# Two dense feed-forward stages as eight fixed slots on four banks, started inside the Fourier attention

## The chip, the cores and the metric

The kernel runs on one core of a Trainium2 chip. The metric is the device time of one execution in microseconds (us); the median of three runs of the kernel before is 939.75 us (938.83 to 942.45).

## The reference, cut to what matters

Four layers, each an attention part and a feed-forward part, act on a sequence of 2048 tokens of 128 features, in fp32. The change touches the end of the last layer: its attention uses Fourier features, and two dense feed-forward networks of 512 hidden units follow, each behind a layer norm.

```python
# layer 3, attention part (x is layer-normed before it, and normed again inside)
p = einsum('blhd,dm->blhm', q_or_k, proj_mat) / sqrt(D_HEAD)
features = concatenate([cos(p), sin(p)]) / sqrt(D_KMAP)       # for keys and for queries
attended = linear_attention(features_q, features_k, v) @ wo + bo
z = z + attended                                              # z: the inner residual
# dense network 1: ln2 with its gain and bias, w1 128x512, w2 512x128
z = z + relu(ln(z) @ w1 + b1) @ w2 + b2
x = x + z
# layer 3, feed-forward part: dense network 2
x = x + relu(layernorm(x) @ W1 + b1) @ W2 + b2                # W1 128x512, W2 512x128
```

## The kernel before, in words

**Tiling.** The 2048 tokens are four chunks of 512 (`NC = 4`, `CH = 512`). All activations stay in SBUF: `X` and `Z` hold the residuals with tokens on partitions, `XH` and `XL` the normed input turned (features on partitions). Every matmul operand is split into a rounded high part (fp32r) and a low remainder, and a product is three matmuls of 128x128 by 128x512 (`mm3`, L695 to L697): high by high, high by low, low by high.

**Stages.** The order of work is written out by hand. `STAGES_` names ten stages, `slots()` runs each over the four chunks, and each engine walks the same list (`walk` for TensorE, ScalarE and VectorE, a loop of its own for GpSimd). A stage's body has named points at which the norm steps of a chunk that is needed two chunks later and the tail of the chunk before are put in; for four-block stages `STEPS_AT[4]` says where. Each engine runs its list strictly in order and waits on semaphores.

**The last Fourier products.** `lin_pe`, `lin_act` and `lin_dve` work through 64 pairs of feature blocks (`PALL = 64`): phases into `gate_banks` or `up_banks`, rounding and subtracting on VectorE (L1606), two Sin activations (L1616, L1617), and products into `route_bank` or `spread_bank` (L1557). After the last pair ScalarE copies the bank out (`output_act`, L1747), VectorE splits it (`project_dve`), TensorE multiplies by `wo3` into `y_bank` (`project_pe`), and ScalarE writes `YT` (`project_act`, L1757). At the end of `lin_pe` and `lin_act` this is done for the last chunk before the next stage begins.

**The dense stages before (FFN3, FFN4).** Each has four hidden blocks of 128 for each chunk (`ffn_pe`, `ffn_act`, `ffn_dve`, `ffn_pool`). A block is: up product into `G[n % 2]` (the two halves of `gate_banks`); ScalarE Relu with bias into `AO[n % 2]` (L864); VectorE CAST to the high part in `rbuf` (L924); GpSimd, and VectorE for the last two blocks of a stage, subtract to get the low part (`low`, L949); down product into `y_bank`, two blocks behind the up product (`lag = 2`). After four blocks ScalarE writes `YT` (`result`, L878), TensorE turns it in four 128x128 transposes into `norm_bank` (`TN`; `tail_pe`, L709), and VectorE adds it to `Z` and `X` (`tail_dve`, L717 to L722). The two sets of everything (two banks, two `AO`, two high and two low buffers) bind a block to the block two before it.

**The norm of a chunk.** Statistics of `Z` or `X` on VectorE (L375, L378), the reciprocal root on GpSimd (L477, L478), normalising into `XN` on VectorE (L395, step 1), four transposes into `norm_bank` (`front_pe`, L662, step 2), a copy to `X32` on ScalarE (L499 with scale and bias, L502 without), then the split into `XH` and `XL` on VectorE (L410, L412, step 3). Norms and tails share `norm_bank`, so the transposes of a norm wait until VectorE has added the tail before (`res_done`), and those of a tail wait for the `X32` copy of the norm before.

## Time and profile before

| | us |
|---|---|
| median of three runs | 939.75 |
| lowest, highest | 938.83, 942.45 |
| the profiled execution's own time | 939.33 |
| its span (first to last instruction) | 937.5 |
| TensorE busy | 749.5 (80%) |
| VectorE busy | 694.7 (74%) |
| ScalarE busy | 553.9 (59%) |
| GpSimd busy | 429.6 (46%) |

The profile shows one execution. A busy share is an average over ten stages with different limits. The granted TensorE clock is given as a share of full speed, and it has two levels, 1.2 and 2.4 GHz; its mean over the span is 0.891. The last Fourier products end shortly before 848.5 us, and the dense stages take the rest of the span.

### The profile page before, as it was taken

What the parts mean: (1) busy time and instruction counts of PE and PEld (TensorE: products, weight loads), DVE (VectorE), ACT (ScalarE), POOL (GpSimd) and SP (SyncE); (2) the same over time, 40 slices, a digit from 0 to 9 for tenths busy, and PEclk for the clock granted to TensorE, in tenths of its full rate; (3) what the DMA queues carried; (4) which work ended last, traced back from release to release, by engine and by line L of the source; (5) the groups of instructions that cost most, each with busy time, mean ns of one, the idle gap of its engine ahead of it and who ended that gap; (6) DMA issues with size and microseconds to landing.
All of it is one profiled execution on the core that took longest, in us unless ns stands there. A gap on an engine that the chain in (4) does not pass through costs nothing. (4 is left out here: it accounts for less than half of the span.)

```text
span 937.5 us, 10990 instructions
## 1 busy us (share of the span) xinstructions
PE 749.5 (80%) x3306; PEld 474.2 (51%) x3306; DVE 694.7 (74%) x1644; ACT 553.9 (59%) x877; POOL 429.6 (46%) x463
## 2 busy tenths in 40 slices
PE   4788996898988799886579888868677867767776
PEld 3566763454655577764456665633232222224554
DVE  6686875989896377776766667778888778784675
ACT  5254664746745356543136666768799887784333
POOL 6547655454442045556426766624433123303554
PEclk9998999979877689999769999978899888898799
DMA  4100000001000000001000000000000000000001
GB/s 137 58 12 15 23 15 25 23 16 31 23 8 11 1 1 1 0 1 34 1 0 1 1 1 0 1 0 1 1 1 0 1 1 0 1 1 0 1 0 46
DMA packets 9610, 11.59 MB, mean 12 GB/s; under 512 B 720, under 2 KB 5712, under 8 KB 9552
## 3 DMA queue, kind: packets, MB, share of 16 engines
q1 hardware_dynamic: 9552, 10.89, 4.0%
q8 instruction: 27, 0.44, 0.2%
q14 instruction: 31, 0.25, 0.1%
HBM read 9.84 MB, written 1.05 MB: 12 GB/s over the span
## 5 line engine op out<-in xcount | busy, mean ns | idle before, releaser
L949 POOL TENSOR_TENSOR rbuf<-B,rbuf 128x512 fp32r<-128x512 f32 x154 | 200.6, 1305 | 175.6 <-ACT rbuf L872 111.2
L917 DVE TENSOR_TENSOR B<-B,spread_bank 128x512 f32<-128x512 f32 x128 | 87.1, 682 | 45.2 <-ACT B L864 35.2
L872 ACT ACTIVATE rbuf<-B 128x512 fp32r<-128x512 f32 x132 | 82.9, 628 | 41.5 <-PE y_bank L697 32.4
L695 PE MATMUL y_bank<-rbuf,WH 128*128 128x512 f32 x174 | 75.5, 434 | 29.8 <-POOL rbuf L949 18.8
L864 ACT ACTIVATE B<-gate_banks,WR 128x512 f32<-128x512 f32 x96 | 66.0, 688 | 39.1 <-PE gate_banks L697 29.0
L904 DVE TENSOR_TENSOR B<-B,up_banks 128x512 f32<-128x512 f32 x68 | 46.5, 684 | 49.0 <-PE up_banks L697 30.1
L861 ACT ACTIVATE B<-gate_banks 128x512 f32<-128x512 f32 x68 | 40.8, 599 | 64.6 <-PE gate_banks L697 63.5
L695 PE MATMUL gate_banks<-XH,WH 128*128 128x512 f32 x168 | 75.5, 450 | 2.5 <-ACT YT L1273 0.8
L477 POOL TENSOR_SCALAR small<-small 128x4 f32<-128x4 f32 x36 | 7.5, 209 | 141.0 <-DVE small L378 140.4
L697 PE MATMUL y_bank<-rbuf,WL 128*128 128x512 f32 x174 | 70.2, 404 | 0.0
L696 PE MATMUL y_bank<-rbuf,WH 128*128 128x512 f32 x174 | 70.2, 404 | 0.0
L697 PE MATMUL gate_banks<-XH,WL 128*128 128x512 f32 x168 | 70.0, 417 | 0.0
L696 PE MATMUL gate_banks<-XL,WH 128*128 128x512 f32 x168 | 70.0, 416 | 0.0
L1616 ACT ACTIVATE B<-B,VEC 128x1024 f32<-128x1024 f32 x48 | 55.3, 1151 | 22.4 <-DVE B L1611 22.3
L1163 POOL TENSOR_SCALAR B<-S,WR 128x128 f32<-128x128 f32 x64 | 39.1, 627 | 50.2 <-DVE S L1145 38.0
L1518 POOL TENSOR_SCALAR WH<-WK 128x512 fp32r<-128x512 f32 x22 | 13.8, 628 | 105.3 <-issue 57.9
L695 PEld LDWEIGHTS y_bank<-rbuf,WH 128*128 128x128 f32 x174 | 33.9, 195 | 55.7 <-POOL rbuf L949 28.7
L1204 PEld LDWEIGHTS spread_bank<-VB,B 128*128 128x128 f32 x256 | 38.2, 229 | 35.7 <-issue 26.5
L823 PE MATMUL spread_bank<-SCT,WE 128*128 128x512 f32 x96 | 42.5, 443 | 11.1 <-DVE B L917 9.2
L1617 ACT ACTIVATE B<-B 128x1024 f32<-128x1024 f32 x48 | 50.5, 1053 | 0.0
L1181 PE MATMUL gate_banks<-B,S 128*64 128x512 f32 x128 | 44.7, 788 | 6.8 <-issue 3.8
L662 PE MATMUL norm_bank<-WR,XN 128*128 128x128 f32 x128 | 22.5, 304 | 32.4 <-DVE XN L395 24.0
(290 smaller groups left out, 2060.3 us busy)
## 6 DMA issues: line engine op xcount, KB each, us to landing
STG<-in_w_split SPq DMA_DIRECT2D x27, 256.0 KB, 2.7
X<-in_x SPq DMA_DIRECT2D x4, 256.0 KB, 6.0
out<-X SPq DMA_DIRECT2D x4, 256.0 KB, 2.3
WR<-in_w_raw SPq DMA_DIRECT2D x1, 524.5 KB, 5.5
STG<-in_w_exact SPq DMA_DIRECT2D x2, 256.0 KB, 2.7
STG<-in_w_split SPq DMA_DIRECT2D x5, 64.0 KB, 1.9
STG<-in_w_split SPq DMA_DIRECT2D x1, 192.0 KB, 2.3
STG<-in_w_split SPq DMA_DIRECT2D x1, 128.0 KB, 2.1
```

Source lines behind the costliest of these rows:

```text
L695: nc.tensor.matmul(dst, w[0], x[0], start=start, stop=False)
L696: nc.tensor.matmul(dst, w[0], x[1], start=False, stop=False)
L697: return nc.tensor.matmul(dst, w[1], x[0], start=False, stop=stop)
L823: nc.tensor.matmul(SP[:, :], WE[:, o:o + P], SCT[:, bass.ds(c % 2 * CH, CH)], start=True, stop=True).then_inc(spread_full, 1)
L864: nc.scalar.activation(AO[n % 2], G[n % 2][:, :], ACT.Relu, bias=raw(bias, b, 1))\
L872: nc.scalar.activation(rbuf[n % 2][:, :], HO[n % 3], ACT.Copy).then_inc(hh_ready, 1)
L904: nc.vector.tensor_tensor(MO[n % 2], AO[n % 2], U[n % 2][:, :], ALU.mult).then_inc(mul_done, 1)
L917: nc.vector.tensor_tensor(HO[n % 3], src, SP[:, :], ALU.mult).then_inc(h_ready, 1)
L949: e_.tensor_tensor(rbuf[2 + n % 2][:, :], AO[n % 2] if f.dense else HO[n % 3], rbuf[n % 2][:, :].bitcast(F32), ALU.subtract).then_inc(hl_r ...
L1181: i = nc.tensor.matmul(G[u][w * WIN:(w + 1) * WIN, :], QN[c_ % 2][:, tok], KM[tile % 2][:, HU * u:HU * u + HU, w * WIN:(w + 1) * WIN], sta ...
L1616: nc.scalar.activation(CS[p % 4], AB[p % 4], ACT.Sin, scale=-TURN, bias=half_pi).then_inc(cos_ready, 1)
L1617: nc.scalar.activation(SN[p % 4], RB[p % 4], ACT.Sin, scale=-TURN).then_inc(sin_ready, 1)
```

## The change

FFN3 and FFN4 leave the general `ffn_` functions. Eight slots of their own (`ring3`, `ring4`; j = 0 to 7) take their place, one for each chunk of each stage, with blocks numbered k = 0 to 31 throughout.

- Up products go round four banks (`UPD`: both halves of `gate_banks` and `up_banks`), and high parts, plain activations and low parts have four buffers each (`HID`, `AOD`, `LOD`); the down product runs three blocks behind, and the output alternates between `spread_bank` and `y_bank` (`YD`).
- ScalarE reads the up bank twice: Relu straight to the rounded high part (`HID`), then Relu in fp32 (`AOD`). The CAST on VectorE is gone. VectorE subtracts for three blocks of a slot and GpSimd for the fourth (VectorE for all four in the last two slots).
- Each slot has one fixed order for norm and tail: on TensorE four blocks, then the norm's transposes, then the tail's; on VectorE low 0, statistics, low 1, the split of the norm before, normalising, low 2, low 3 where it has it, tail.
- The first two up products are issued ahead of the last Fourier products, the next two behind them, and the attention's last projection and its copy move into slot 0.
- Norms from (7, 2) on are turned in `route_bank` (`R`) instead of `norm_bank`; the wait on `res_done` goes, and the tails no longer wait for these norms' `X32` copies.

```diff
-    _f.lag = 2 if _f.dense else 3
+    _f.lag = 3
+        def norm_bank(n, c):
+            return R if count(n, c) >= count(7, 2) else TN
...
-                if turned["tails"]:
+                if norm_bank(n, c) is R:
+                    pe.wait_ge(oq_read, NC)
+                elif turned["tails"]:
                     pe.wait_ge(res_done, turned["tails"])
...
-                pe.wait_ge(x32_ready, turned["norms"])
+                pe.wait_ge(x32_ready, min(turned["norms"], count(7, 2)))
...
+                if p == PALL - 1:
+                    for k in range(2):
+                        ring_up(pe, k)
                 lin_use(pe, p)
...
-            if cp == 2 * NC - 1:
-                project_pe(pe, NC - 1)
...
                 output_act(a, NC - 1)
-                project_act(a, NC - 1)
...
+        DEEP, RB4 = 4, 4
+        UPD = [G[0], G[1], U[0], U[1]]
+        AOD = [buf[0], buf[1], buf[2], buf[3]]
+        HID = [SCT[:, 0:CH], SCT[:, CH:2 * CH], rbuf[2][:, :], rbuf[3][:, :]]
+        LOD = [WE[:, 0:CH], WE[:, CH:2 * CH], rbuf[0][:, :], rbuf[1][:, :]]
+        YD = [SP, Y]
+        SLOTS = 2 * NC
...
+        def ring_front(j):
+            return divmod(count(7, 2) + j, NC) if count(7, 2) + j < count(9, 0) else None
+        def ring_tail(j):
+            return divmod(count(6, NC - 1) + j, NC)
+        def ring_low_on_pool(k):
+            return k % RB4 == 3 and k // RB4 < SLOTS - 2
+        def ring_up(pe, k):
...
+            if k < DEEP:
+                pe.wait_ge(r_ready, PALL - 1 + k // 2)
+            else:
+                pe.wait_ge(act_done, n - DEEP + 1)
+            mm3(UPD[n % DEEP][:, :], wh(f.up, b * P), (chunk(XH, c, PAD), chunk(XL, c, PAD)), True, True)\
+                .then_inc(first_full, 1)
...
+        def ring_pe(pe, j):
+            for b in range(RB4):
+                k = RB4 * j + b
+                if k >= 2:
+                    ring_up(pe, k)
+                if k == 3:
+                    project_pe(pe, NC - 1)
+                if k >= 3:
+                    ring_down(pe, k - 3)
+            if ring_front(j):
+                front_pe(pe, *ring_front(j), 2)
+            tail_pe(pe, *ring_tail(j))
+            if j == SLOTS - 1:
+                for k in range(RING - 3, RING):
+                    ring_down(pe, k)
+        def ring_act(a, j):
...
+                a.wait_ge(first_full, n + 1)
+                if k >= DEEP:
+                    a.wait_ge(down_done, n - DEEP + 1)
+                nc.scalar.activation(HID[n % DEEP], UPD[n % DEEP][:, :], ACT.Relu, bias=bias).then_inc(hh_ready, 1)
+                if k >= DEEP:
+                    a.wait_ge(hl_ready, n - DEEP + 1)
+                elif k == 0:
+                    a.wait_ge(pair_used, PALL - 3)
+                nc.scalar.activation(AOD[n % DEEP], UPD[n % DEEP][:, :], ACT.Relu, bias=bias).then_inc(act_done, 1)
+                if b == 0 and j:
+                    if ring_front(j - 1):
+                        front_act(a, None, *ring_front(j - 1), 2)
+                if b == 2:
+                    if j:
+                        result(j - 1)
+                    else:
+                        project_act(a, NC - 1)
...
+        def ring_low(e_, eng, k):
...
+            e_.tensor_tensor(LOD[n % DEEP], AOD[n % DEEP], HID[n % DEEP].bitcast(F32), ALU.subtract)\
+                .then_inc(hl_ready, 1)
+        def ring_dve(v, chain, j):
+            front, last = ring_front(j), ring_front(j - 1) if j else None
+            for b in range(RB4):
+                if not ring_low_on_pool(RB4 * j + b):
+                    ring_low(nc.vector, v, RB4 * j + b)
+                if b == 0 and front:
+                    front_dve(v, chain, *front, 0)
+                if b == 1:
+                    if last:
+                        front_dve(v, chain, *last, 3)
+                    if front:
+                        front_dve(v, chain, *front, 1)
+            tail_dve(v, chain, *ring_tail(j))
+        def ring_pool(g, chain, j):
+            if ring_front(j):
+                front_pool(g, chain, *ring_front(j), 0)
+            if ring_low_on_pool(RB4 * j + 3):
+                ring_low(nc.gpsimd, g, RB4 * j + 3)
```

## Rows read from the trace of the kernel before

**Rows 1.** Busy time by engine in stretches (us, busy with count, PEclk, DMA share, GB/s)
```profile
848.40:934.90 86.50, 64.97 (x257) 46.20 (x255) 55.96 (x135) 32.39 (x48) 44.85 (x40) 0.89 0.03 10
...
872.00:876.00 4.00, 2.09 (x7) 1.90 (x8) 2.22 (x6) 0.78 (x1) 1.27 (x1) 0.59 0.00 0
...
916.00:920.00 4.00, 2.01 (x12) 1.68 (x12) 2.86 (x7) 1.30 (x3) 2.06 (x2) 1.00 0.24 68
```

**Rows 2.** Who waited for whom, 852 to 937.5: total us, times, longest
```profile
ACT B L864 <- POOL rbuf L949: 9.6, 6, 2.2
...
PE norm_bank L662 <- DVE X L720: 5.4, 2, 2.7
```

**Rows 3.** Timeline of the dense stages, moments of several slots: start, duration, [idle before <-releaser]
```profile
864.66 0.43 DVE L410 CAST XH<-X 128x512 fp32r<-128x512 f32 x1 [1.23 <-ACT X L499]
...
865.12 0.69 DVE L412 TENSOR_TENSOR XL<-X,XH 128x512 fp32r<-128x512 f32 x1
...
866.07 0.86 DVE L375 BATCH_NORM_STATS2 small<-Z 128x6 f32<-128x128 f32 x4
...
866.96 0.38 DVE L378 BATCH_NORM_AGGREGATE small<-small 128x2 f32<-128x6 f32 x4
...
867.92 1.01 POOL L478 TENSOR_TENSOR small<-small,VEC 128x4 f32<-128x4 f32 x1
...
870.38 2.06 DVE L395 TENSOR_SCALAR XN<-Z,small 128x128 f32<-128x128 f32 x4
...
873.91 1.08 PE L662 MATMUL norm_bank<-WR,XN 128*128 128x128 f32 x4 [2.71 <-DVE X L720]
...
876.31 0.69 ACT L864 ACTIVATE B<-gate_banks,WR 128x512 f32<-128x512 f32 x1 [0.50 <-PE gate_banks L697]
...
879.75 0.60 PE L709 MATMUL norm_bank<-WR,YT 128*128 128x128 f32 x4
...
881.08 0.69 ACT L864 ACTIVATE B<-gate_banks,WR 128x512 f32<-128x512 f32 x1 [1.52 <-PE gate_banks L697]
...
891.46 1.72 POOL L478 TENSOR_TENSOR small<-small,VEC 128x4 f32<-128x4 f32 x1
...
893.79 1.11 DVE L395 TENSOR_SCALAR XN<-X,small 128x128 f32<-128x128 f32 x4
```

**Rows 4.** Groups by line and shape from 846 on, ACT, DVE and POOL: busy, mean ns | idle
```profile
L864 ACT ACTIVATE B<-gate_banks,WR 128x512 f32<-128x512 f32 x32 | 22.1, 689 | 29.1 <-PE gate_banks L697 19.4 <-POOL rbuf L949 9.6
...
L499 ACT ACTIVATE X<-norm_bank,WR 128x512 f32<-128x512 f32 x2 | 1.6, 778 | 5.9 <-PE norm_bank L662 5.9
...
L502 ACT ACTIVATE X<-norm_bank 128x512 f32<-128x512 f32 x4 | 2.4, 596 | 8.2 <-PE norm_bank L662 8.2
...
L924 DVE CAST rbuf<-B 128x512 fp32r<-128x512 f32 x32 | 16.9, 530 | 20.4 <-ACT B L864 14.1 <-PE y_bank L697 6.3
...
L949 POOL TENSOR_TENSOR rbuf<-B,rbuf 128x512 fp32r<-128x512 f32 x28 | 36.2, 1295 | 62.8 <-DVE rbuf L924 62.8
```

**Rows 5.** Timeline of the end
```profile
930.90 0.69 DVE L949 TENSOR_TENSOR rbuf<-B,rbuf 128x512 fp32r<-128x512 f32 x1
...
934.14 0.69 DVE L722 TENSOR_TENSOR X<-X,norm_bank 128x512 f32<-128x512 f32 x1 [1.94 <-PE norm_bank L709]
```

**Rows 6.** Chain of waits: one matmul of a running row at the low clock
```profile
875.42 0.43 PE gate_banks L696
```

**Rows 7.** Timeline of the last Fourier products
```profile
841.89 1.22 DVE L1606 SCALAR_TENSOR_TENSOR S<-S,up_banks 128x1024 f32<-128x1024 f32 x1 [0.17 <-ACT S L1593]
...
845.07 0.78 PE L1557 MATMUL route_bank<-S,KVT 128*32 128x512 f32 x1 [1.05 <-ACT S L1616]
...
848.47 0.60 ACT L1747 ACTIVATE STG<-route_bank 128x512 f32<-128x512 f32 x1 [2.51 <-PE route_bank L1557]
...
853.91 0.69 ACT L864 ACTIVATE B<-gate_banks,WR 128x512 f32<-128x512 f32 x1 [1.79 <-PE gate_banks L697]
```

**Rows 8.** Line L878 from 840 on: duration ns, first and last start
```profile
L878 ACT ACTIVATE YT<-y_bank,WR x8: 687/687/688, 865.3 to 932.7; 128x512 f32<-128x512 f32 x8
```

More of the change, by code:

```diff
@@ L883, in ffn_act @@
                     hook(LATE_ROUTE)
-                if not f.dense:
-                    for at_ in lagged(f, c, b, 2 if f.gate else 1):
-                        high(*at_)
+                for at_ in lagged(f, c, b, 2 if f.gate else 1):
+                    high(*at_)
                 if c and b == f.lag - 1:
@@ L934, in ffn_dve @@
                         weigh(*at_)
-                elif f.dense:
-                    split(c, b)
                 else:
                     weigh(c, b)
-                if not f.dense and (c, b) == (NC - 1, f.blocks - 1):
+                if (c, b) == (NC - 1, f.blocks - 1):
                     for k in (2, 1):
@@ L959, in ffn_pool @@
             for b in range(f.blocks):
-                for at_ in lagged(f, c, b, 0 if f.dense else 2):
+                for at_ in lagged(f, c, b, 2):
                     if low_on_pool(f, *at_):
@@ L1800, in walk @@
             for body, c, tail, norm, route in slots():
-                was_late, late = late, body == "scan" or isinstance(body, Ffn) and body.dense
+                if body in RINGS:
+                    j = c + NC * RINGS.index(body)
+                    ring_dve(eng, chain, j) if which == 2 else (ring_pe, ring_act)[which](eng, j)
+                    continue
+                was_late, late = late, body == "scan"
                 late_norm = norm if not late else route if was_late else None
```

80 lines of the change are left out of this document (57 added, 23 removed), and 1 row of the table STEPS_AT.

## The prediction

> **What bounds the kernel now.** Only the end of the span changes, so I read the busy times by stretch first. From 848.4 to 934.9 us TensorE is busy for 65 of 86.5 us at a mean granted clock of 0.89, VectorE for 56, GpSimd for 45, ScalarE for 32 [rows 1]: no engine fills the stretch, and it is a chain of waits. The list of waits says which: ScalarE's Relu waits for GpSimd's subtraction, because two buffers tie a block to the one two before (9.6 us in 6 waits), and twice the norm's transposes wait 2.7 us until VectorE has added a tail, because both use one bank [rows 2]. The timeline shows the second at 873.91, with the clock low behind it: 0.59 granted from 872 to 876 [rows 1, 3]. The groups give the price of one instruction: Relu 0.69, result 0.69, `X32` copy 0.78 with scale (0.60 without), GpSimd's subtraction 1.30 [rows 4], VectorE's 0.69 [rows 5].
>
> **The change part by part.** I follow one slot. In steady state TensorE issues 24 matmuls of 512 columns and eight transposes. A matmul in a running row takes 0.43 us at the low clock [rows 6], about half of that at the high one: 5.2 us, some 6 with transposes. ScalarE has eight Relu, a copy and a result: 8x0.69+0.6+0.69 = 6.8 us. VectorE has three subtractions (2.1), statistics (866.07 to 867.34, 1.27), the split (864.66 to 865.81, 1.15), normalising 1.11 and the tail 0.7 or 1.4: 6.3 to 7.0 us [rows 3]. So no engine needs more than 7.0 us. But the fixed order closes a longer loop, which I take as the limit. From the end of normalising:
>
> - transposes of the norm, then of the tail, then the next slot's first up product. The tail's transposes and an up product take 1.33 us to the start of Relu (879.75 to 881.08) [rows 3]; for the norm's own I add 0.4 and for handing over 0.07: 1.8 us;
> - two Relu, 1.4 us: 3.2;
> - low 0 with its hand-over 0.76: 3.95; statistics 1.27: 5.2; low 1, which may wait for its Relu for 0.1: 6.0; split 1.15: 7.2; normalising 1.11: 8.3 us.
>
> GpSimd's reciprocal root runs beside low 1 and the split. From the end of statistics to its end it takes 1.6 us (867.34 to 868.93), against 1.94 for what hides it: nothing. But it took 1.72 instead of 1.01 us at 891.46 [rows 3]; with that, and low 1 and split both in its way, the loop is 9.0. I take 8.7, the middle. The tail's addition, low 2 and GpSimd's low 3 lie in the 3.2 us in which VectorE waits otherwise. The result of the slot before is written 3.6 us after the second Relu, long before it is turned: the third block of lag, the second output bank and the extra buffers cost nothing here.
>
> In each round TensorE is done with its blocks about 2.3 us before the norm arrives (8.7 less 0.8 for transposes and 5.6 for the matmuls with their start). Before, a pause of 2.71 us ended in the low clock (873.91), while one of two us did not (916 to 920, granted 1.00) [rows 1, 3]. At the low clock the norm's transposes and an up product take 2.40 us to the start of Relu (873.91 to 876.31) instead of 1.33; with the tail's four transposes more the loop grows by 1.4 us. I give each round half of it, 0.7. Bounds per round: 8.3 at no loss, 10.4 at full loss and the slow root.
>
> **The start.** The two early up products are six matmuls, 1.4 to 2.6 us, set before the last pair's products. Their banks are free at 843.11 (841.89+1.22) [rows 7], and TensorE had a pause of 1.05 us just before 845.07; so the last products come 0.3 to 1.5 us later, and I take 1.0. ScalarE's copy-out then starts at 849.5 instead of 848.47 and ends at 850.1; two Relu end at 851.5 (before, the first Relu began at 853.91 [rows 7]); low 0 ends at 852.25, statistics 853.55, the root 1.6 to 2.3 us later, say 855.4, and normalising 856.5. The attention's projection and its result lie beside that: the split of the copied bank (1.15 us, as the split above) ends at 851.3, and low 0, queued behind it on VectorE, can't begin before 851.5. The projection waits for that split on TensorE with down product 0 behind it, which needs low 0 anyway. Behind a pause of over 3 us the loop's second half costs 3.2+1.4: the second Relu of slot 1 ends at 861.1.
>
> **The end.** Rounds from slot 1 to slot 6 are five: 861.1+5x8.7+5x0.7 = 908.1. Slots 6 and 7 have no norm to make, so ScalarE's 6.8 us bind from 6 to 7: 914.9. After the second Relu of slot 7 come six Relu and a result, 7x0.69 = 4.85: 919.8; the last low 0.76: 920.5. From the end of the last low to the end of the span it was 937.5-931.59 = 5.9 us, by the same steps [rows 5]: 926.4. So the span falls by 11.1 us. The profiled execution took 939.33 (1.83 around its span), which becomes 928.2; it lies 0.4 under the median, so against the median I forecast 928.6.
>
> A price that speaks against the change: ScalarE does eight passes in a slot instead of four, to save VectorE casts of 0.43 us when free (530 ns in the mean [rows 4]) with Relus of 0.69. The Trainium skill, page "ScalarE: Activation LUTs", section "Rules for kernel authors", tells to do relu on VectorE and not on ScalarE. No row here shows a Relu on VectorE; by that rule the second pass is dear. By the rows it is 4x0.69 = 2.8 us a slot on an engine that is busy for 32 of 86.5 us; only two Relu of a slot are in the loop, and one Relu more and one cast less lengthen it by 0.26.
>
> **The rivals.**
>
> A, the loop is no limit, because the norm comes early enough, and ScalarE binds at 6.9 us a slot. For it: without a norm in the slot, only 6.8 us of work stand in line. Against it: the sum of the loop holds no guess greater than 0.4. It gives, without the clock's 1.4 at the start and with the 18.3 us from slot 6 to the end of the sum above (6.8+4.85+0.76+5.9), 859.7+5x6.9+18.3 = 912.5, a time of 914.7. Chance 0.08.
>
> B, GpSimd's low 3 meets the normalising. Normalising took 2.06 us when a subtraction of GpSimd ran beside it (870.38) and 1.11 alone (893.79) [rows 3]. In the loop low 3 is ready six ScalarE passes, a copy and a result behind the second Relu, 5.7 us, and normalising ends 5.1 to 5.8 us behind it: a late root brings them together, each round gets 0.95 more and the clock falls each time. 926.4+4.8+3.5 = 934.7, a time of 936.9. Chance 0.12. The Trainium skill, page "SBUF — State Buffer", section "Who interferes with whom", has it that whichever of the two starts first holds their shared port for the whole instruction. By that rule the loss per meeting is up to one subtraction, 1.3 us, and could fall on GpSimd instead.
>
> C, the clock stays at 1.2 GHz, since every round holds a pause: the side on which it is slower. Then TensorE needs 24x0.43 = 10.3 and about 0.9 for each four transposes (1.08 with their end at 873.91 [rows 3]), 12.1 us a slot. For it: the pause is there in each round. Against it: a slower TensorE fills its own pause, and 0.89 was granted with longer ones [rows 1]. 861.1+5x12.1 = 921.6, then 11.3 for slot 6 to 7 and some 15 to the end: 948, a time of 950. It is slower from a round of 11.6 us on. Chance 0.06.
>
> D, it doesn't do what it says: the rounds keep their pace. From the first result to the last were seven steps of 9.6 us (865.3 to 932.7 [rows 8]); with the new start, a first result at 864.7 and 5 us behind the last, it ends at 937: no change. For it: norm, tail and up stay in one chain. Against it: the waits of [rows 2] have lost what they wait for: the bank is another, and the buffers are four. Chance 0.08.
>
> **How the numbers follow.** The forecast has 0.66. Its own range: at best (start 0.7 earlier and no slow root, rounds of 8.3, no loss of clock but the first) 918.5, so 920.7; at worst (start 0.8 later, rounds of 10.4, one loss more at the end) 933.6, so 935.8. A is below it; B and D reach above it, and I take the range to 938 to hold most of them: 919 to 938. What a measurement of this kernel can tell from no change is about 0.5%, 4.7 us. Faster by more, under 935.05: the forecast, A and half of B, 0.80. Within: half of B and most of D, 0.13. Slower: C and a little of D, 0.07.
>
> **What would show it.** Right: in the new trace the norm's transposes go to `route_bank`, wait for `XN`, never for a tail's addition; the distance of second Relus of slots' first blocks is 8.3 to 10.4 us in slots 1 to 6 and near 7 from 6 to 7; ScalarE has 64 Relus near 0.69 in the stretch; the copy-out of the last Fourier chunk starts 0.3 to 1.5 us later. Wrong: rounds near 7 us (A), normalising of 2 us beside GpSimd in most slots (B), a granted clock near 0.5 in the whole stretch (C), or any difference ahead of 842 us, where no instruction changes.

## The result: faster, and by twice the forecast

The changed kernel takes 914.9 us (median of four runs, 913.16 to 922.16), the kernel before beside it 939.29 (937.31 to 942.45): a ratio of 0.976 (95% interval 0.973 to 0.979). That is 24.4 us less where 11 were forecast, and below the forecast's range.

The head of the page, span and busy times of the changed kernel:

```profile
span 913.8 us, 11022 instructions
...
PE 736.8 (81%) x3306; PEld 468.5 (51%) x3306; DVE 686.2 (75%) x1634; ACT 568.6 (62%) x909; POOL 401.1 (44%) x441
```

VectorE and GpSimd are busy for 9 and 29 us less, ScalarE for 15 more: the casts and most of GpSimd's subtractions are gone, the second Relu pass has come. TensorE has as many matmuls as before and is busy for 13 us less; 11.8 of them (62.2 for 74.0 us, 295 matmul records each) lie in the part from the addition described next to the end, where the granted clock is 0.97 instead of 0.87.

**A measure for small differences.** Kernels that are identical up to the Fourier attention reach its last part at different times. The last addition to `Z` before the last Fourier products stands here, once of each kernel (start, duration, [idle time before]):

```profile
835.00 0.69 DVE L717 TENSOR_TENSOR Z<-Z,norm_bank 128x512 f32<-128x512 f32 x1 [2.16 <-PE norm_bank L709]
```

```profile
833.45 0.69 DVE L721 TENSOR_TENSOR Z<-Z,norm_bank 128x512 f32<-128x512 f32 x1 [2.15 <-PE norm_bank L713]
```

Among the fourteen profiles it starts anywhere from 827.98 to 840.84 us, with not one instruction changed ahead of it, and the whole times scatter with it. So beside each ratio I give the **stretch**, from the start of this addition to the end of the span. It was 102.5 us before (937.5-835.00) and is 80.35 after (913.8-833.45): 22.15 us less, the whole gain but for the 1.55 us of an earlier start. Each stretch comes from one profiled execution. For the changed kernel two executions agree (`after_again`); for the others nothing says how much it scatters.

The stages by stretch, columns as in [rows 1]. Just before, from 836 to 842 us, the granted clock is still between 0.50 and 0.88; from 842 us to the end of the last matmuls it is 1.00 in every two microseconds, where the dense stages had 0.89 in the mean before, and 0.59 in [rows 1] at the lowest:

```profile
844.00:846.00 2.00, 2.00 (x14) 0.55 (x14) 0.00 (x0) 0.44 (x2) 0.00 (x0) 1.00 0.00 0
848.00:852.00 4.00, 1.57 (x6) 0.83 (x6) 2.78 (x13) 3.76 (x7) 1.55 (x2) 1.00 0.00 0
872.00:876.00 4.00, 3.53 (x16) 2.50 (x14) 3.73 (x14) 4.00 (x8) 1.61 (x2) 1.00 0.00 0
896.00:900.00 4.00, 4.00 (x19) 3.04 (x18) 2.47 (x5) 4.00 (x8) 0.00 (x0) 1.00 0.23 66
845.96:911.06 65.10, 53.01 (x249) 40.57 (x249) 46.54 (x125) 47.15 (x80) 17.42 (x18) 1.00 0.05 13
```

The list of waits from 846 us on. ScalarE no longer waits for GpSimd, and the norm's transposes wait for the norm, never for a tail's addition; both waits of [rows 2] are gone:

```profile
ACT SCT L1844 <- PE gate_banks L701: 14.4, 7, 2.7
...
PE route_bank L666 <- DVE XN L397: 9.4, 6, 3.1
...
DVE XN L397 <- POOL small L480: 2.1, 6, 1.2
```

The groups by line and shape, which answer to [rows 4]: 64 Relus in place of 32, no cast, six subtractions on GpSimd in place of 28:

```profile
L1844 ACT ACTIVATE SCT<-gate_banks,WR 128x512 fp32r<-128x512 f32 x16 | 11.1, 693 | 14.5 <-PE gate_banks L701 14.4
L1849 ACT ACTIVATE B<-gate_banks,WR 128x512 f32<-128x512 f32 x16 | 11.1, 693 | 0.0
```

```profile
L1870 POOL TENSOR_TENSOR rbuf<-B,rbuf 128x512 fp32r<-128x512 f32 x6 | 7.7, 1286 | 11.5 <-DVE rbuf L1870 11.5
```

And one full round in the timeline, from one `XN` to the next (the rows answer to [rows 3]):

```profile
875.73 1.12 DVE L397 TENSOR_SCALAR XN<-X,small 128x128 f32<-128x128 f32 x4 [0.18 <-POOL small L480]
...
876.90 0.66 PE L666 MATMUL route_bank<-WR,XN 128*128 128x128 f32 x4 [1.37 <-DVE XN L397]
...
877.75 0.48 PE L699 MATMUL gate_banks<-XH,WH 128*128 128x512 f32 x1
...
878.73 0.69 ACT L1844 ACTIVATE SCT<-gate_banks,WR 128x512 fp32r<-128x512 f32 x1 [2.26 <-PE gate_banks L701]
...
879.31 0.68 ACT L1849 ACTIVATE B<-gate_banks,WR 128x512 f32<-128x512 f32 x1
...
880.08 0.69 DVE L1870 TENSOR_TENSOR WE<-B,SCT 128x512 fp32r<-128x512 f32 x1 [0.63 <-ACT B L1849]
...
880.36 0.70 ACT L1844 ACTIVATE SCT<-gate_banks,WR 128x512 fp32r<-128x512 f32 x1
...
880.69 0.87 DVE L377 BATCH_NORM_STATS2 small<-X 128x6 f32<-128x128 f32 x4
...
880.93 0.71 ACT L1849 ACTIVATE B<-gate_banks,WR 128x512 f32<-128x512 f32 x1
...
881.59 0.38 DVE L380 BATCH_NORM_AGGREGATE small<-small 128x2 f32<-128x6 f32 x4
...
881.89 0.66 DVE L1870 TENSOR_TENSOR WE<-B,SCT 128x512 fp32r<-128x512 f32 x1
...
882.06 0.54 POOL L479 TENSOR_SCALAR small<-small 128x4 f32<-128x4 f32 x1 [3.16 <-DVE small L380]
...
882.68 1.07 POOL L480 TENSOR_TENSOR small<-small,VEC 128x4 f32<-128x4 f32 x1
...
883.79 1.12 DVE L397 TENSOR_SCALAR XN<-X,small 128x128 f32<-128x128 f32 x4 [0.17 <-POOL small L480]
```

Read downwards it is the forecast loop: `XN`, four transposes, the up product, two Relus, low 0, statistics, root, `XN` again, 8.06 us. TensorE idles for 1.37 us ahead of the transposes and ScalarE for 2.26 ahead of its first Relu; that is where the two wait for the loop. From the second Relu of a slot's first block to that of the next (all eight ends: 847.72, 855.71, 863.82, 871.93, 879.99, 888.05, 896.46, 902.54) the rounds are 7.99, 8.11, 8.11, 8.06, 8.06, 8.41 and, from slot 6 to 7, 6.08 us.

### The profile page after: what moved, and what is told of

Read it like the earlier page. It is cut to its first block and busy times, and to the rows that moved or that the text cites. A ratio compares the mean times of both kernels' runs of the same rounds, so it can differ in the third digit from the quotient of the medians.

```text
span 913.8 us, 11022 instructions
## 1 busy us (share of the span) xinstructions
PE 736.8 (81%) x3306; PEld 468.5 (51%) x3306; DVE 686.2 (75%) x1634; ACT 568.6 (62%) x909; POOL 401.1 (44%) x441
## 3 DMA queue, kind: packets, MB, share of 16 engines
HBM read 9.84 MB, written 1.05 MB: 12 GB/s over the span
## 5 line engine op out<-in xcount | busy, mean ns | idle before, releaser
L937 POOL TENSOR_TENSOR rbuf<-B,rbuf 128x512 fp32r<-128x512 f32 x126 | 164.4, 1307 | 111.2 <-ACT rbuf L873 109.7
L699 PE MATMUL y_bank<-rbuf,WH 128*128 128x512 f32 x150 | 63.9, 426 | 21.9 <-POOL rbuf L937 14.5
L699 PE MATMUL gate_banks<-XH,WH 128*128 128x512 f32 x152 | 66.5, 437 | 0.8 <-ACT YT L1261 0.8
L701 PE MATMUL gate_banks<-XH,WL 128*128 128x512 f32 x152 | 62.1, 409 | 0.0
L700 PE MATMUL gate_banks<-XL,WH 128*128 128x512 f32 x152 | 61.8, 407 | 0.0
L701 PE MATMUL y_bank<-rbuf,WL 128*128 128x512 f32 x150 | 60.3, 402 | 0.0
L700 PE MATMUL y_bank<-rbuf,WH 128*128 128x512 f32 x150 | 60.1, 401 | 0.0
L865 ACT ACTIVATE B<-gate_banks,WR 128x512 f32<-128x512 f32 x64 | 43.9, 686 | 10.0 <-PE gate_banks L701 9.7
L699 PEld LDWEIGHTS y_bank<-rbuf,WH 128*128 128x128 f32 x150 | 29.2, 195 | 40.2 <-POOL rbuf L937 21.5
L397 DVE TENSOR_SCALAR XN<-X,small 128x128 f32<-128x128 f32 x96 | 39.1, 469 | 8.0 <-POOL small L480 6.5
```

Of the source, the lines that this page charges most:

```text
L397: i = nc.vector.tensor_scalar(dst(j), src[:, c * TL + j, :], mv[:, j, 0:1], rs[:, j:j + 1], ALU.subtract, ALU.mult)
L699: nc.tensor.matmul(dst, w[0], x[0], start=start, stop=False)
L700: nc.tensor.matmul(dst, w[0], x[1], start=False, stop=False)
L701: return nc.tensor.matmul(dst, w[1], x[0], start=False, stop=stop)
L865: nc.scalar.activation(AO[n % 2], G[n % 2][:, :], ACT.Relu, bias=raw("b1_2", b, 1))\
L937: e_.tensor_tensor(rbuf[2 + n % 2][:, :], HO[n % 3], rbuf[n % 2][:, :].bitcast(F32), ALU.subtract).then_inc(hl_ready, 1)
```

## The experiments

Each shows its edit against the changed kernel, unless it says otherwise. "Round" is the distance just defined, in slots 0 to 7.

| kernel | median us (runs) | before beside it | ratio, 95% interval | stretch us |
|---|---|---|---|---|
| `after_again` | 917.86 (6) | 941.32 | 0.974, 0.971 to 0.978 | 80.35 |
| `late_ups` | 920.84 (6) | 941.32 | 0.979, 0.975 to 0.983 | 83.4 |
| `tn_bank` | 933.54 (12) | 941.32 | 0.991, 0.988 to 0.994 | 96.6 |
| `stats_early` | 915.76 (6) | 941.32 | 0.973, 0.968 to 0.977 | 78.4 |
| `before_bank` | 936.35 (10) | 941.16 | 0.996, 0.993 to 0.999 | 99.7 |
| `pause` | 922.44 (4) | 941.16 | 0.984, 0.980 to 0.988 | 87.5 |
| `early_both` | 910.61 (6) | 941.16 | 0.970, 0.967 to 0.974 | 74.5 |
| `two_banks` | 919.68 (4) | 941.16 | 0.982, 0.978 to 0.987 | 80.3 |
| `low3_late` | 907.64 (6) | 937.37 | 0.969, 0.964 to 0.973 | 72.2 |
| `low_dve` | 917.41 (4) | 937.37 | 0.980, 0.976 to 0.984 | 80.0 |
| `cast_dve` | 923.57 (4) | 937.37 | 0.985, 0.981 to 0.989 | 85.4 |
| `tail_first` | 913.47 (4) | 937.37 | 0.975, 0.972 to 0.979 | 77.8 |

`after_again` was measured beside the rows that have 941.32 in the third column; the others have a "before" of their own. Ratio and stretch point the same way for most rows, but the size can differ: `two_banks`, `low_dve` and `tail_first` read 0.001 to 0.008 more than its 0.974 and have stretches that are equal or shorter, with intervals that still meet it. Differences under some 1% rest on the stretches alone.

**after_again**, the changed kernel once more. Expected:

> The changed kernel once more, as the measure for the other three beside it. If its ratio of 0.976 to the kernel before is a property of the kernel, it comes back within 0.973 to 0.979. Theory 1 (the round): the dense stages are set by a round of 8.1 us through VectorE's order (normalising, transposes, up product, two Relu, low 0, statistics, root), at a granted clock of 1.00 throughout; the rounds are 8.0 to 8.4 again. Theory 2 (the clock was luck): the clock falls in some rounds in this execution, rounds of 9.5 us turn up, and the ratio moves to 0.98 or above.

Measured: 0.974, and a stretch of 80.35 us, the same to a hundredth, while the addition that opens it came 4.0 us later (837.45). The rounds are the same to 0.01 us too, and the clock is 1.00 again, as theory 1 had it.

**late_ups**, the two early up products behind the last Fourier products again.

```diff
-                if p == PALL - 1:
-                    for k in range(2):
-                        ring_up(pe, k)
...
-                if k >= 2:
-                    ring_up(pe, k)
+                ring_up(pe, k)
```

> The first two up products are issued behind the last Fourier products instead of ahead of them; all else stays. Theory A (the early ups fill a pause of TensorE and keep its clock up): the last twelve Fourier products run at the low clock again, 3.4 us to the copy-out of the bank instead of 1.9, and two ups (1.4 us at the high clock, 2.6 at the low) stand between them and the first Relu, of which the copy-out covers 0.6: 1.5 to 3.5 us slower than the changed kernel. Theory B (the rise of the clock there was chance, the ups cost what they save): the copy-out comes up to 1.4 us earlier, the first Relu at the same time or 0.8 us later: within 1 us of the changed kernel.

Measured: stretch 3.05 us longer. The copy-out of the last Fourier chunk starts 13.51 us behind the addition; before the change it was 13.47, in the changed kernel 12.51. So the early products don't delay it by the 1.0 us that I gave them, they bring it forward by 1.0. The timelines show how. With the products late TensorE pauses for 1.06 us and its last four matmuls take 1.94 us; with them early it has no pause, and the same four take 1.03:

```profile
843.21 0.80 PE L1545 MATMUL route_bank<-S,KVT 128*32 128x512 f32 x1 [1.06 <-ACT S L1604]
...
844.65 1.94 PE L1545 MATMUL route_bank<-S,KVT 128*32 128x512 f32 x4
...
846.63 0.60 ACT L1731 ACTIVATE STG<-route_bank 128x512 f32<-128x512 f32 x1 [2.52 <-PE route_bank L1545]
```

```profile
842.41 0.49 PE L699 MATMUL gate_banks<-XH,WH 128*128 128x512 f32 x1
...
844.01 0.62 PE L1545 MATMUL route_bank<-S,KVT 128*32 128x512 f32 x1
...
844.89 1.03 PE L1545 MATMUL route_bank<-S,KVT 128*32 128x512 f32 x4
...
845.96 0.60 ACT L1734 ACTIVATE STG<-route_bank 128x512 f32<-128x512 f32 x1 [1.56 <-PE route_bank L1545]
```

The windows say that it is the clock: from 844 to 846 us 0.50 without them, 1.00 with them (above).

```profile
844.00:846.00 2.00, 2.00 (x12) 0.33 (x4) 0.00 (x0) 0.10 (x1) 0.00 (x0) 0.50 0.00 0
```

The other 2.05 us lie between copy-out and the second Relu of slot 1, 11.8 instead of 9.75 us. Of these 0.6 come before `XN` (it starts 6.08 us behind the copy-out instead of 5.49), since slot 0's products are late, and 1.46 behind it, at the low clock: TensorE pauses for 2.71 us, the granted clock is 0.50 from 854 to 856 us, and the transposes take 1.11 instead of 0.66 us.

```profile
853.88 1.11 PE L666 MATMUL route_bank<-WR,XN 128*128 128x128 f32 x4 [2.71 <-DVE XN L397]
```

All later rounds are the same to 0.01 us. Theory A holds, with 3.05 in its 1.5 to 3.5 us.

**tn_bank**, the norms turned in the tail's bank again, so that they wait for the tail's addition, the tail ahead of the front.

```diff
-            return R if count(n, c) >= count(7, 2) else TN
+            return TN
...
-                pe.wait_ge(x32_ready, min(turned["norms"], count(7, 2)))
+                pe.wait_ge(x32_ready, turned["norms"])
...
+            tail_pe(pe, *ring_tail(j))
             if ring_front(j):
                 front_pe(pe, *ring_front(j), 2)
-            tail_pe(pe, *ring_tail(j))
```

> Norms and tails share one bank again. The tail's transposes go ahead of the norm's (the other order would wait for itself), and the norm's wait until VectorE has added the tail. Theory 1 (the bank matters because the round runs through it): behind normalising VectorE does low 2 (0.7) and the tail (1.4, in the last stage 0.7) before the norm can be turned, while the tail's own transposes leave the round (0.35 less): +1.0 to +1.8 us in each of six rounds, 6 to 11 us slower than the changed kernel, more if the longer pause of TensorE lets the clock fall. Rival (the gain is in buffers and order, the bank was no limit): within 2 us.

Measured: stretch 96.6, 16.2 us more, rounds of 9.72, 11.35, 11.25, 11.83, 11.47, 9.4 and 6.09. The timeline shows the norm's transposes held by the addition in the bank, though `XN` is long there (it starts at 894.08), and the windows a clock that falls behind such pauses:

```profile
894.08 1.12 DVE L397 TENSOR_SCALAR XN<-X,small 128x128 f32<-128x128 f32 x4 [0.17 <-POOL small L480]
...
897.92 1.08 PE L666 MATMUL norm_bank<-WR,XN 128*128 128x128 f32 x4 [3.16 <-DVE X L724]
```

```profile
876.00:880.00 4.00, 4.00 (x13) 3.13 (x12) 1.58 (x7) 2.16 (x4) 0.00 (x0) 0.57 0.02 4
896.00:900.00 4.00, 2.08 (x7) 1.91 (x8) 1.74 (x2) 0.00 (x0) 1.23 (x1) 0.59 0.00 0
```

The five rounds from slot 1 to 6 grow by 2.9 us in the mean (11.06 for 8.15), of which up to some 1.4 may be TensorE at the low clock, by the prediction's steps and the 1.46 of `late_ups`. That is more than the 6 to 11 us of theory 1, which left room for the clock. Without the bank all else, the early products with it, is worth 5.9 us of 22.15. This edit changes the bank and the order of the transposes; `tail_first` below has the order alone, and against its 77.8 the bank costs 18.8 us.

**before_bank**, from the other side: the kernel before with nothing but the other bank for the norms.

```diff
+        def norm_bank(n, c):
+            return R if count(n, c) >= count(7, 2) else TN
...
-                if turned["tails"]:
+                if norm_bank(n, c) is R:
+                    pe.wait_ge(oq_read, NC)
+                elif turned["tails"]:
                     pe.wait_ge(res_done, turned["tails"])
...
-                    i = nc.tensor.transpose(TN[:, j * P:(j + 1) * P], XN[:, j, :], ident)
+                    i = nc.tensor.transpose(norm_bank(n, c)[:, j * P:(j + 1) * P], XN[:, j, :], ident)
...
-                pe.wait_ge(x32_ready, turned["norms"])
+                pe.wait_ge(x32_ready, min(turned["norms"], count(7, 2)))
```

> The kernel before with one part of the change alone: norms from (7, 2) on are turned in the route bank, without the wait for the tail's addition. Theory 1 (each part is worth what its waits show): the two pauses of 2.7 us and the one of 2.0 behind a tail's addition go, with the low clock behind the first two, which cost 1.4 each: 5 to 9 us faster than before, 930 to 935 where that takes 940. Theory 2 (the fixed order and the four buffers are the gain, the bank only makes them possible): the norm comes no earlier, since normalising itself ends late behind GpSimd's subtraction: 0 to 3 us.

Measured: 0.996, stretch 99.7, 2.8 us less, as theory 2 had it (0 to 3). The wait for the addition is gone, but the next one is 1.3 us for `XN` itself, which takes 2.06 us beside GpSimd's subtractions:

```profile
869.37 2.06 DVE L398 TENSOR_SCALAR XN<-Z,small 128x128 f32<-128x128 f32 x4
...
871.49 0.94 PE L667 MATMUL route_bank<-WR,XN 128*128 128x128 f32 x4 [1.30 <-DVE XN L398]
```

So the bank alone gives 2.8, everything without the bank 5.9, both together 22.15 us. They aren't a sum. I read it so that each part removes one of the waits that hold the same loop, and that with either left the loop stays long and the clock falls in its pauses; the three numbers are measured, this reason for them is argued.

**pause**: two passes more on VectorE, over a 128x512 table (0.88 us together), between the split and normalising, so that `XN` comes later.

```diff
                     if front:
+                        sc_ = SC2[:, :, :].rearrange("p t k -> p (t k)")
+                        for _ in range(2):
+                            chain(nc.vector.tensor_scalar(sc_, sc_, 1.0, 0.0, ALU.mult, ALU.add))
                         front_dve(v, chain, *front, 1)
```

> Two passes of VectorE over an unused 128x512 tile (about 0.5 us each with their waits) are added in each slot between the split and normalising; they compute nothing that is read. They lengthen the round, and TensorE's pause before the norm's transposes from 1.4 to about 2.4 us. Theory 1 (the round goes through VectorE): +1.0 us in each of six rounds, 6 us slower than the changed kernel, clock at 1.00. Theory 2 (the pause also decides the clock): the clock falls in some rounds as with the shared bank, each of these +1.4 more: 8 to 15 us slower. Rival (VectorE has slack): under 2 us.

Measured: stretch 7.15 us longer, rounds of 8.11, 10.24, 8.77, 8.94, 9.51, 10.18 and 6.19 us. Where the clock holds, from 868 to 880 us, the round is 8.77, 0.7 more, which is the added work less the 0.17 us that `XN` waited anyway; the two rounds of over ten us are those whose transposes are slow. Their pauses are no longer than others: 1.10 (862.37) and 2.04 us ahead of slow transposes, 2.01, 2.09 and 3.17 ahead of fast ones (0.66 us for four at 1.00, 1.11 at the low clock). The clock also fell behind the fast transposes at 881.33, to 0.84 and 0.73 from 880 to 888 us; those are the rounds of 8.94 and 9.51. Two of the sets and their windows:

```profile
872.60 0.66 PE L666 MATMUL route_bank<-WR,XN 128*128 128x128 f32 x4 [2.01 <-DVE XN L397]
...
899.77 1.11 PE L666 MATMUL route_bank<-WR,XN 128*128 128x128 f32 x4 [2.04 <-DVE XN L397]
```

```profile
872.00:876.00 4.00, 3.40 (x19) 2.96 (x20) 2.74 (x7) 1.56 (x3) 1.29 (x1) 1.00 0.00 0
900.00:904.00 4.00, 4.00 (x16) 3.49 (x16) 1.01 (x2) 0.94 (x2) 1.27 (x1) 0.60 0.15 44
```

In the changed kernel a pause of 3.05 us, the longest, cost nothing at all:

```profile
852.62 0.66 PE L666 MATMUL route_bank<-WR,XN 128*128 128x128 f32 x4 [3.05 <-DVE XN L397]
```

So what I assumed, that a pause of over two us is followed by the low clock, holds in some rounds and fails in others. The kernel before held a case against it that I overlooked: 0.87 us of pause, slow transposes behind it, and 0.50 granted from 908 to 910 us.

```profile
906.74 1.07 PE L662 MATMUL norm_bank<-WR,XN 128*128 128x128 f32 x4 [0.87 <-DVE XN L395]
```

The loss is real where it comes (10.2 for 8.8, 1.4 us a round), but the length of the one pause doesn't predict it. What does stays open. The stretch lies between theory 1 (6 us slower) and theory 2 (8 to 15); the falling clock is theory 2's.

**two_banks**: the up products on two banks in place of four.

```diff
-        UPD = [G[0], G[1], U[0], U[1]]
+        UPD = [G[0], G[1], G[0], G[1]]
...
-            if k < DEEP:
+            if k < 2:
                 pe.wait_ge(r_ready, PALL - 1 + k // 2)
             else:
-                pe.wait_ge(act_done, n - DEEP + 1)
+                pe.wait_ge(act_done, n - 2 + 1)
```

> Up products go round two banks instead of four; buffers and order stay. Theory 1 (depth costs nothing and gives little): an up product must wait for the second Relu of the block two before, which ScalarE has done when TensorE gets there in the middle of a slot; only the start loses, since the third and fourth up product no longer run beside the copy-out: 0.5 to 2.5 us slower than the changed kernel. Theory 2 (four banks are what makes the gain): ScalarE idles an up product's 1 us in most blocks, 2 us or more in each round, 15 us slower.

Measured: stretch 80.3, rounds equal to 0.02 us, so not even the 0.5 to 2.5 us of theory 1. By this profile the four banks are worth nothing in this order. The ratio of the whole times reads 0.982 with an interval that barely meets that of `after_again`, and the profiled execution was the fastest of the four (911.99 us, the others 917.34 to 925.36). I go by the stretch, which leaves out the scatter ahead of it; that the other three had the same stretch is not shown.

**stats_early**: the next slot's statistics right behind the tail's addition, not behind low 0.

```diff
             if cp == 2 * NC - 1:
+                front_dve(v, chain, *ring_front(0), 0)
                 project_dve(v, NC - 1)
...
                 if b == 0 and front:
-                    front_dve(v, chain, *front, 0)
-                if b == 1:
-                    if last:
-                        front_dve(v, chain, *last, 3)
-                    if front:
-                        front_dve(v, chain, *front, 1)
+                    front_dve(v, chain, *front, 1)
+                if b == 1 and last:
+                    front_dve(v, chain, *last, 3)
             tail_dve(v, chain, *ring_tail(j))
+            if j + 1 < SLOTS and ring_front(j + 1):
+                front_dve(v, chain, *ring_front(j + 1), 0)
```

> On VectorE the statistics of a norm move from behind low 0 of their slot to the end of the slot before (for the first, ahead of the split of the last Fourier chunk), and normalising follows low 0 at once, with low 1 and the split of the norm before behind it. Theory 1 (the round through VectorE's order is the limit): statistics, root and low 1 (about 1.2+1.8 us with what they hide) leave the round, and the next limits are the work of TensorE and VectorE in a slot, 6.4 to 6.6 us: rounds of 6.5 to 6.9 instead of 8.1, 6 to 9 us faster than the changed kernel, near 906 to 909 where that takes 915. Rival (ScalarE or TensorE's own work sets the round already): no gain, within 1.5 us.

Measured: stretch 78.4, but with rounds of 5.59, 7.44, 8.29, 8.48, 8.46, 8.48 and 6.08: faster at first, then slower than the 8.06 that they replace. Only 1.95 us are gained where the theory had 6 to 9. The timeline shows the new loop. The tail's addition, now ahead of the statistics, runs beside GpSimd's low 3 and takes 1.38 instead of 0.69 us, the root is delayed, and `XN` waits 1.18 us for it. The addition and the root's wait, both beside the loop before, are in it now:

```profile
871.30 1.30 POOL L1871 TENSOR_TENSOR rbuf<-B,rbuf 128x512 fp32r<-128x512 f32 x1 [3.59 <-DVE rbuf L1871]
...
871.77 1.38 DVE L724 TENSOR_TENSOR X<-X,Z 128x512 f32<-128x512 f32 x1
...
876.23 1.11 DVE L397 TENSOR_SCALAR XN<-X,small 128x128 f32<-128x128 f32 x4 [1.18 <-POOL small L480]
```

**early_both**: statistics early as in `stats_early`, the split of the last norm also directly behind low 0, ahead of normalising, and on TensorE the tail's transposes ahead of the norm's (the swap shown for `tn_bank`).

```diff
-                if b == 0 and front:
-                    front_dve(v, chain, *front, 0)
-                if b == 1:
+                if b == 0:
                     if last:
                         front_dve(v, chain, *last, 3)
...
```

> Statistics of the next norm at the end of a slot on VectorE, the split of the last norm and normalising directly behind low 0, and on TensorE the tail's transposes ahead of the norm's. With the statistics alone moved, rounds stayed at 8.5 us, since they now stood behind the tail, and the tail behind the norm's transposes. Theory (a round through norm and tail together): with the tail turned first, the tail, statistics and root run ahead of the norm; what is left is work: TensorE 6.4 us, VectorE 6.6 in the third layer's network, ScalarE 5.8. Rounds of 6.5 to 7.0 instead of 8.1, 70 to 73 us from the tail's addition to Z at 833 to the end of the span, where the changed kernel takes 80.4; 7 to 10 us faster than it. Rival (transposes, hand-overs and the shared port of VectorE and GpSimd already fill the round): rounds of 7.8 or more, under 2 us.

Measured: stretch 74.5, ratio 0.970; rounds 6.04, 7.45, 6.71, 7.2, 7.68, 7.7 and 6.09. By the stretch it is 5.8 us faster than the changed kernel, between the theory (7 to 10) and the rival (under 2). The addition still meets low 3 in the later rounds:

```profile
876.31 1.30 POOL L1871 TENSOR_TENSOR rbuf<-B,rbuf 128x512 fp32r<-128x512 f32 x1 [2.75 <-DVE rbuf L1871]
...
876.77 1.38 DVE L724 TENSOR_TENSOR X<-X,Z 128x512 f32<-128x512 f32 x1
```

**low3_late**: `early_both`, and GpSimd's low 3 waits for the tail's addition.

```diff
             if ring_low_on_pool(RB4 * j + 3):
+                g.wait_ge(res_done, count(*ring_tail(j)) + 1)
                 ring_low(nc.gpsimd, g, RB4 * j + 3)
```

> The kernel with early statistics and the tail turned first, and one more wait: GpSimd's low 3 begins only when VectorE has added the tail, so that it runs beside the statistics (one input from SBUF) and not beside the second addition of the tail (two inputs), which took 1.38 us instead of 0.69 there. Theory (the two engines shut each other out, and the addition is in the round): 0.5 to 0.7 us less in each of the rounds that were 7.2 to 7.7: 71 to 72.5 us from the tail's addition to Z before the last Fourier products to the end of the span, where it was 74.5 (80.4 in the changed kernel, 102.5 in the kernel before). Rival (low 3 then holds up low 0 and the root behind it, so the time only moves): 74 to 76.

Measured: stretch 72.2, the shortest; rounds 6.04, 7.44, 6.71, 6.52, 6.86, 7.03 and 6.08; the addition takes 0.69 us again, and low 3 follows it, as the theory had it (71 to 72.5 us):

```profile
880.98 0.69 DVE L724 TENSOR_TENSOR X<-X,Z 128x512 f32<-128x512 f32 x1
...
881.75 1.29 POOL L1871 TENSOR_TENSOR rbuf<-B,rbuf 128x512 fp32r<-128x512 f32 x1 [4.04 <-DVE X L724]
```

It beats the kernel before: 907.64 against 937.37 us beside it, 0.969 (0.964 to 0.973). Against the changed kernel it is 8.2 us by the stretch, 0.9%; its interval just touches that of the changed kernel's first measurement (0.973 to 0.979) and overlaps that of `after_again`, so the whole times alone don't show it. The Trainium skill, page "SBUF — State Buffer", section "Who interferes with whom", says that a VectorE operation with two SBUF inputs and one of GpSimd that reads SBUF exclude each other, the later one waiting. The trace agrees: 1.38 us beside GpSimd's 1.30, 0.69 alone; in `stats_early` low 3 ends at 872.60, and the addition that began at 871.77 ends 0.55 us behind it.

**low_dve**: low 3 on VectorE like the others.

```diff
-        return k % RB4 == 3 and k // RB4 < SLOTS - 2
+        return False
```

> The changed kernel with all four subtractions of a slot on VectorE, none on GpSimd. Theory (the fourth was off the round): VectorE waits about 0.6 us for the tail's transposes and 0.6 for the next slot's Relu in each round; the fourth subtraction, 0.6, fits there: 80 to 81 us from the tail's addition to Z to the end, as in the changed kernel (80.4). Rival (VectorE's work is the limit): 0.6 us in each round, 84 us.

Measured: stretch 80.0, as the theory had it; rounds 8.0, 8.12, 8.1, 8.05, 8.06, 8.05, 6.09. Only the last round of a norm is shorter (8.05 for 8.41). So low 3 on GpSimd is neither a gain nor, as rival B had it, a loss in the changed kernel's order: it lies in the part of the round in which VectorE waits.

**cast_dve**: one Relu on ScalarE and the cast of its result on VectorE, as before the change, in the slots' order.

```diff
-                nc.scalar.activation(HID[n % DEEP], UPD[n % DEEP][:, :], ACT.Relu, bias=bias).then_inc(hh_ready, 1)
...
-            eng.wait_ge(act_done, n + 1)
...
             for b in range(RB4):
+                n = FFN3.block0 + RB4 * j + b
+                v.wait_ge(act_done, n + 1)
+                if n >= FFN3.block0 + DEEP:
+                    v.wait_ge(down_done, n - DEEP + 1)
+                nc.vector.tensor_copy(HID[n % DEEP], AOD[n % DEEP]).then_inc(hh_ready, 1)
```

> The changed kernel with ScalarE reading each up bank once: VectorE makes the high part by a CAST of the activation, as the kernel before did, instead of a second Relu on ScalarE. Theory (the round counts instructions on its path, not passes of ScalarE): one Relu leaves the path (0.57), two casts enter it (0.43 each), the other two fit into VectorE's waits: +0.3 to +0.6 a round, 82 to 84 us from the tail's addition to Z to the end (80.4 in the changed kernel). Rival (a second pass on ScalarE is dear, relu belongs on VectorE's side of the work): without 32 passes of 0.6 it is faster, under 79.

Measured: stretch 85.4, 5.05 us more and beyond the theory's 82 to 84; from one `XN` to the next 8.7 to 9.1 us (873.16, 882.27, 890.98, 899.69), with the clock below 1.00 in several stretches, and a pause of 2.03 us ahead of the transposes:

```profile
873.16 1.11 DVE L397 TENSOR_SCALAR XN<-X,small 128x128 f32<-128x128 f32 x4
...
874.32 0.69 PE L666 MATMUL route_bank<-WR,XN 128*128 128x128 f32 x4 [2.03 <-DVE XN L397]
```

```profile
876.00:880.00 4.00, 4.00 (x14) 3.10 (x13) 3.57 (x10) 1.87 (x3) 1.03 (x1) 0.72 0.00 0
```

The theory had two of the casts fit into VectorE's waits; they don't, since VectorE has hardly any left. It is busy for 3.90 of each 4 us from 888 to 900 us, at a granted clock of 1.00, where `XN` follows `XN` at 8.71 us. So the round is set there by all of VectorE's work, 0.65 us longer than in the changed kernel; what the clock adds in other rounds was not separated. Against 4 casts of 0.42 us a slot the pass on ScalarE pays. The rule of the Trainium skill that the prediction weighed ("ScalarE: Activation LUTs", "Rules for kernel authors"), relu on VectorE, was not run; what was run says that a cast moved to VectorE is dear here, where VectorE's order is the loop and its time is nearly full.

**tail_first**: only the swap on TensorE, the tail's transposes ahead of the norm's.

> The changed kernel with only the order of the two sets of transposes on TensorE swapped: the tail's before the norm's. Theory (the tail's transposes stand in the round between the norm's and the next up product): 0.4 us less in each of six rounds, 77.5 to 78.5 us from the tail's addition to Z to the end (80.4 in the changed kernel). Rival (the root or VectorE's tail closes a round of the same length elsewhere): 80 to 80.7.

Measured: stretch 77.8, as the theory had it; rounds 7.56, 7.68, 7.67, 7.62, 7.63, 7.96 and 6.09. Each norm's round is 0.44 us shorter: the tail's transposes run while TensorE waits for `XN` anyway, instead of between the norm and the up product.

## Where the prediction was right, and where it failed

The span was to be 926.4 and is 913.8: 12.6 us less, in these parts.

| part | forecast | measured | difference |
|---|---|---|---|
| unchanged code ahead | as in the trace | 1.55 earlier | 1.55 |
| copy-out, from there | 1.0 later | 1.0 earlier | 2.0 |
| copy-out to second Relu of slot 1 | 11.6 | 9.75 | 1.85 |
| five rounds | 47.0 | 40.75 | 6.25 |
| slot 6 to 7 | 6.8 | 6.08 | 0.7 |
| Relus and result of slot 7 | 4.85 | 4.51 | 0.35 |
| the rest to the end | 6.66 | 6.75 | -0.1 |

**The mechanism was right.** The round is the loop through VectorE's order that the prediction followed, and its bare sum of 8.3 us stands against 8.0 to 8.1 measured. `tail_first` shortens the round by what it takes off that loop, `pause` lengthens it by what it adds, while `two_banks` and `low_dve`, which leave the loop alone, change nothing. The waits went as forecast, the norm's transposes to `route_bank` among them, and `XN` was never slower than 1.12 us. Rival A (rounds of 6.9 by ScalarE) and rival C (the clock at 1.2 GHz) are refuted by the rounds and by the granted 1.00; B by `XN` at 1.12 us and by `low_dve`; D by the rounds themselves, though `tn_bank`, with 11.06, shows what it would have been with the bank shared.

Rival A gave a time of 914.7 us, and the median is 914.9. That is chance: A's mechanism, rounds of 6.9 us that ScalarE binds, isn't there. Its five rounds would be 34.5 us and are 40.75, and a later start and a longer end in its sum make up for it.

Of the signs that the prediction named for being right, three were missed in size: the rounds of slots 1 to 6 were to be 8.3 to 10.4 us (only the last, 8.41, is), the one from 6 to 7 near 7 (6.08), and the copy-out was to come later (it comes 1.0 us earlier). A difference ahead of 842 us, a sign of being wrong, is there with 1.55 us, but executions of the changed kernel alone differ by 4.0 at that point.

**The step that failed** is "I give each round half of it, 0.7": the loss of clock behind the pause in each round. It is 3.5 us over five rounds, 1.4 behind the pause in the start. All of it was nought in the two executions profiled: the granted clock stayed at 1.00 from 842 us on, and each of the six sets of norm's transposes took 0.66 us, behind pauses of 0.44 to 3.05 us. The premise behind the step, that a pause of over two us brings the low clock, doesn't hold: 3.05 us kept the clock, while 0.87 us in the kernel before did not. The size of the loss was right: 1.46 us in `late_ups`, 1.4 in `pause`. `pause` also shows that a round only 0.7 us longer does lose it now and then. Half the loss in each round was an average over two outcomes, and in the changed kernel only one of them came; why it did stays open.

**The start** had the wrong sign, too. I counted the six matmuls of the early products as work ahead of the last Fourier products, and gave the 1.05 us pause only as a deduction. `late_ups` measures it: they fill the pause, so that the last products begin 0.5 us later, not 1.0; the clock stays up, and from the first of the twelve matmuls to the copy-out it takes 1.95 instead of 3.42 us. They finish 1.0 us sooner. That is 2.0 us of the sum.

**The slow root** was a term of 0.4 us a round, as the middle between 8.3 and 9.0. The root did come behind a small operation of GpSimd (0.54 us where it was 0.20 alone), but ended 1.78 us behind the statistics, and `XN` waited 0.17 us for it. Beyond that the round of 8.06 above is some 0.2 us under the bare sum: two Relus take 1.26 from the start of the first to the end of the second (priced 1.4), low 1 ends 0.58 behind the statistics (priced 0.79), these take 1.20 (priced 1.27), and the other steps come to 0.2 more. Such steps overlap their neighbours: a Relu records 0.69 to 0.72 us, but the next starts 0.57 to 0.59 behind it, as at 878.73 and 879.31 in the round above, and low 1 starts at 881.89, before the statistics' recorded end at 881.97. In slot 7 I priced seven passes in a row by the recorded time, 4.85; they took 4.51. From slot 6 to 7, where the prediction had ScalarE bind at 6.8 us, it is TensorE that binds, busy for 4.00 of 4 us from 896 to 900, at 6.08.

**The range** has a slip at its lower end. A start 0.7 us earlier, no slow root and no loss of clock in the rounds make 926.4-0.7-2.0-3.5 = 920.2, a time of 922.4 and not 920.7; the 918.5 comes out nearly (918.8) if the 1.4 behind the first pause is dropped too, which the text keeps.

Where did the gain over my 11 come from, then? Of the 12.6 us some 6.4 are the clock (1.5 in the start, 1.4, 3.5; the last two by my own price for it), 0.5 the early products, priced at twice what they cost, 4.15 the length of rounds and Relus, 1.55 unchanged code, which is no effect of the change. Of the stretch's 22.15 us against before, 3.05 go with the early products (`late_ups`), of which 2.9 are the clock, while 0.6 of an earlier `XN` and 0.5 of later Fourier products nearly cancel, and 16.2 with the bank once the slots are there (`tn_bank`). These shares overlap and are no sum.

## What to carry to other kernels

Follow the loop that closes a fixed order through all its engines, and price it with the starts of neighbouring instructions, not with their recorded durations. Work that fills a pause of TensorE can be worth more than it costs, since it also keeps the clock; where the clock is in doubt, give the two outcomes as two cases, not their mean. What holds one loop in two places has to go in both: here the bank alone gave 2.8 us, all the rest alone 5.9, and both 22.

## What the runs showed that I had not expected

- ScalarE's 128x512 passes from PSUM record 0.69 to 0.73 us but follow each other at 0.57 to 0.59 us, so a row of them is a sixth cheaper than the sum of its records.
- Pauses of TensorE of 3.05 us (changed kernel) and 3.17 (`pause`) left the granted clock at 1.00; pauses of 0.87 (before), 1.10 and 2.04 (`pause`), 2.71 (`late_ups`) and 3.16 us (`tn_bank`) were followed by the low clock, 0.50 to 0.56 in two microseconds behind them.
- GpSimd's 128x4 operation took 0.54 us in place of 0.20 when VectorE's subtraction ran beside it, and normalising, 1.11 to 3.04 us before, took 1.11 to 1.12 in all six slots once GpSimd's subtractions were out of its way.
- With identical instructions ahead, the same point of the program lay up to 12.9 us apart between executions' profiles (827.98 to 840.84). The profiles agree in the number of records ahead of it to one, and differ in the clock: from 200 to 400 us it was granted 0.90 in the two that came first (827.98, 829.88) and 0.82 to 0.83 in the four that came last (837.13 to 840.84). One more with 0.83 came at 834.30, so this goes with the scatter and needn't be all of it; why the clock differs stays open.
